# The first pass of a two-layer graph kernel: another order of the same steps within a slot

## The chip, the cores and the metric

One Trainium2 chip, one core of it. The metric is the time of one launch in device microseconds (us), measured outside of the profile. Several launches are timed and their median is compared.

## What is computed

Two graph layers follow each other over one graph of 3125 nodes and 103125 edges, which are sorted by destination. The change lies in the first, an attention layer with 4 heads of 32 channels:

```python
q = (x @ Wq.T + bq).reshape(N, H, C)
k = (x @ Wk.T + bk).reshape(N, H, C)
v = (x @ Wv.T + bv).reshape(N, H, C)
alpha = jnp.sum(q[dst] * k[src], axis=-1) / np.sqrt(C)
m = jax.ops.segment_max(alpha, dst, num_segments=N)
e = jnp.exp(alpha - m[dst])
z = jax.ops.segment_sum(e, dst, num_segments=N)
a = e / z[dst]
msg = a[:, :, None] * v[src]
out = jax.ops.segment_sum(msg, dst, num_segments=N)
```

Dense layers and norms follow, and then a second layer, which gathers rows again, weighs them with a small network of the edge's length and direction, and sums them by destination. All is in 32-bit floats.

## The kernel before

**Parts.** A short start makes tables of queries and of keys and values in device memory. The *first pass* goes over the edges for the attention layer. Then come the dense layers, then the *second pass* over the edges, and the end. The change touches the first pass alone.

**Tiles and slots.** An edge tile is 128 edges, a quad four tiles (`QT = 4`), and there are 202 quads (`NQ`). Every engine runs its own loop over *slots* `q`, one quad entering in each, and the engines meet at semaphores. A quad goes through this:

- GpSimd gathers the keys and values of its edges' sources (line 436, four gathers of 128 rows each) into a ring of 16 buffers. A buffer is filled again once VectorE has weighed the quad in it.
- SyncE loads the query rows of the quad's destinations (line 342, `windows`: edges are sorted, so 128 rows from the tile's first destination do), four slots ahead, once the queries of four slots ago are done. Every seventh slot it also stores a piece of a radial embedding for the second pass (line 364), for which it waits for an exponential of ScalarE (line 816).
- ScalarE makes one-hot matrices, edge by destination within the window (`make_hots`, lines 735 and 738: four squares and one Relu), three slots ahead.
- TensorE turns them (`turn_hots`, line 484, four transposes), two slots ahead; ScalarE copies the result out of PSUM (`turned`, line 749, into `hotT`); TensorE multiplies them with the query rows (`queries`, line 493), one slot ahead.
- VectorE multiplies queries and keys (`product`, line 1015) and adds up each head's 32 channels (`scores`, line 1025) into `alpha`.
- Quads form batches of eight, of four near the end. When a batch is complete, a chain of small steps works out each destination's maximum and the exponentials. It is spread over four slots, `step` 0 to 3 (`chain_at`): a transpose, two scans and the masks (step 0), two small transposes and scans over a row (step 1), twelve tiny matmuls and two scans (step 2), an exponential and a transpose back (step 3). ScalarE then copies the probabilities out (line 802).
- Twelve slots after it entered (`weighed(q)`), a quad is weighed: ScalarE spreads its probabilities over the channels (`spread`, line 758, into `exb`), and VectorE multiplies the values with them (`weigh`, line 1031, into `msg0`). In four slots (`DOUBLES`) and at the very end two quads are weighed.
- TensorE sums messages and probabilities by destination with the one-hots (`sums`, line 502: eight matmuls of 128x128, two for a tile), into one of two pairs of PSUM banks, and VectorE adds each tile's sums to the accumulator (`add_tile`, line 1046). `added(q)` are the quads weighed in the slot before.

A 32-bit matmul of 128 columns leaves two rows in the trace, a transpose one.

**The order in a slot, before.** Each engine works in the order in which its loop is written. TensorE: sums of the quads weighed in the slot before; the chain's step 0, 1 or 2; turns for slot `q + 2`; queries for slot `q + 1`; the chain's step 3. ScalarE: step 3's exponential; turned copy; small copies of steps 1 and 2; spread; one-hots; copy of the probabilities. VectorE: product; then per quad add 0, scores, add 1, weigh, add 2, the chain's step, add 3.

`sums` waits for `msg_ready` (the weighing) and for `acc_step` (VectorE's adds out of the same PSUM banks two quads ago). `queries` waits for the turned copy, for SyncE's windows and for the product of two quads ago (`prod_ready`). `turn_hots` waits for the one-hots and for the last turned copy.

## Time and profile before

| | |
|---|---|
| median of 3 runs | 3034.0 us (3033.17 to 3050.24) |
| the profiled execution | 3050.12 us |
| its span, first to last instruction | 3048.3 us |
| mean granted TensorE clock | 0.806 |
| first pass, steady stretch | 186 to 1480 us |
| second pass | about 1700 to 2980 us |

The profile is one execution. PE is TensorE's matmuls and PEld its weight loads, DVE is VectorE, ACT ScalarE, POOL GpSimd, SP SyncE. A row names the line, the engine, the operation, the tiles written and read, and what the engine waited for before it (`[5.49 <-remote]`: it stood idle for 5.49 us, and the profile does not know what ended that). "issue" is a wait for which the profile shows nothing. Ends of matmuls are modelled. The granted clock is 1 at 2.4 GHz and 0.5 at 1.2 GHz.

### The profile page before, as it was taken

Reading aid. Unit: us, or ns where it says so; the run is one execution under the profiler, and the core shown is the slowest. Engines: PE = TensorE matmul, PEld = TensorE weight load, DVE = VectorE, ACT = ScalarE, POOL = GpSimd, SP = SyncE. Lnnn points to the kernel's source line nnn. Section 1 sums busy time; section 2 is a strip of 40 time slices with the busy share of each in tenths; the row PEclk is TensorE's granted clock in tenths of the full one; section 3 lists DMA queues with packets and bytes.
Section 4 is the critical chain, followed back from the end, with each engine's and each line's share of the span. In section 5 each row is a group of like instructions: output and inputs, shape, how many; then the busy total and the mean of one; then the engine's idle time right before and its main releaser. Section 6 shows DMA issues by size and latency. Waiting matters only on the chain. (4 is left out here: it accounts for less than half of the span.)

```text
span 3048.3 us, 43625 instructions
## 1 busy us (share of the span) xinstructions
PE 2125.3 (70%) x12777; PEld 1763.9 (58%) x12777; DVE 1697.7 (56%) x4672; ACT 1216.2 (40%) x3032; POOL 1567.9 (51%) x1618
## 2 busy tenths in 40 slices
PE   4266666666666666656688178888888888888886
PEld 3255555565555566555676156666666666666665
DVE  2455555555555555555755055665666665666666
ACT  1344444444444444433435033333343333334344
POOL 4345555555555555545202756665666566656630
PEclk7588888878888878888888578787887777878788
DMA  6344444444343444434201211111111111111110
GB/s 219 86 113 120 120 122 120 117 121 121 113 124 112 124 122 114 115 106 123 77 5 31 52 37 45 45 45 42 46 47 45 42 44 44 45 42 45 46 28 22
DMA packets 212127, 243.01 MB, mean 80 GB/s; under 512 B 42992, under 2 KB 170022, under 8 KB 211508
## 3 DMA queue, kind: packets, MB, share of 16 engines
q0 software_dynamic: 64480, 158.57, 18.8%
q1 hardware_dynamic: 147412, 81.66, 9.3%
q8 instruction: 105, 1.72, 0.2%
q14 instruction: 130, 1.06, 0.1%
HBM read 228.12 MB, written 11.94 MB: 79 GB/s over the span
## 5 line engine op out<-in xcount | busy, mean ns | idle before, releaser
L436 POOL DMA_INDIRECT rows<-kv_tab,src_col x806 | 762.9, 947 | 712.3 <-DVE msg L1031 482.2
L451 POOL DMA_INDIRECT rows<-up_tab,src_col x806 | 791.9, 982 | 520.1 <-DVE hots L1308 272.6
L502 PE MATMUL ps<-hots,msg 128*128 128x128 f32 x1616 | 410.8, 344 | 493.1 <-DVE msg L1031 433.9
L699 PE MATMUL ps<-hotT,hots 128*128 128x128 f32 x3232 | 550.6, 340 | 260.4 <-DVE hots L1315 202.9
L699 PEld LDWEIGHTS ps<-hotT,hots 128*128 128x128 f32 x3232 | 504.2, 246 | 293.1 <-DVE hots L1315 219.1
L502 PEld LDWEIGHTS ps<-hots,msg 128*128 128x128 f32 x1616 | 314.9, 242 | 535.0 <-DVE msg L1031 480.5
L1279 DVE TENSOR_TENSOR acc<-acc,ps 128x256 f32 x808 | 336.6, 417 | 398.1 <-remote 225.1
L749 ACT COPY hotT<-ps 128x512 f32<-128x512 f32 x202 | 118.2, 585 | 815.4 <-remote 434.1
L1046 DVE TENSOR_TENSOR acc<-acc,ps 128x256 f32 x808 | 334.3, 414 | 130.9 <-remote 75.2
L502 PE MATMUL ps<-hots,exb 128*128 128x128 f32 x1616 | 386.3, 329 | 0.0
L1031 DVE TENSOR_TENSOR msg<-rows,exb 128x512 f32<-128x512 f32 x202 | 142.6, 706 | 424.6 <-ACT exb L758 289.9
L502 PEld LDWEIGHTS ps<-hots,exb 128*128 128x128 f32 x1616 | 318.0, 244 | 0.0
L688 PEld LDWEIGHTS ps<-weights,hots 64*128 64x128 f32 x1616 | 208.2, 198 | 104.4 <-issue 104.4
L493 PE MATMUL ps<-qwin,hotT 128*128 128x128 f32 x1616 | 247.8, 302 | 16.9 <-issue 11.6
L735 ACT ACTIVATE hots<-consts,nrel 128x128 f32<-128x128 f32 x808 | 257.6, 391 | 0.0
L735 ACT ACTIVATE hotT<-consts,nrel 128x128 f32<-128x128 f32 x808 | 255.6, 389 | 2.9 <-PE ps L699 2.9
L907 ACT ACTIVATE hots<-ps,vecs 128x512 f32<-128x512 f32 x101 | 69.4, 687 | 460.8 <-PE ps L678 170.7
L688 PE MATMUL ps<-weights,hots 64*128 64x128 f32 x1616 | 248.8, 297 | 5.8 <-issue 5.8
L493 PEld LDWEIGHTS ps<-qwin,hotT 128*128 128x128 f32 x1616 | 231.0, 219 | 18.1 <-issue 17.9
L901 ACT ACTIVATE hots<-ps,vecs 128x512 f32<-128x512 f32 x101 | 69.4, 687 | 378.2 <-PE ps L672 144.7
L1015 DVE TENSOR_TENSOR work<-ps,rows 128x512 f32<-128x512 f32 x202 | 138.0, 683 | 134.2 <-remote 113.5
L484 PE MATMUL ps<-consts,hots 128*128 128x128 f32 x808 | 148.6, 315 | 73.2 <-ACT hots L738 72.4
(163 smaller groups left out, 2569.7 us busy)
## 6 DMA issues: line engine op xcount, KB each, us to landing
qwin<-q_tab SPq DMA_DIRECT2D x808, 64.0 KB
rows<-kv_tab,src_col POOLq DMA_INDIRECT x806
rows<-up_tab,src_col POOLq DMA_INDIRECT x806
hots<-emb_rows SPq DMA_DIRECT2D x202, 16.0 KB
weights<-r_far SPq DMA_DIRECT2D x25, 128.0 KB
emb_rows<-weights SPq DMA_DIRECT2D x25, 128.0 KB
kv_tab<-rows SPq DMA_DIRECT2D x12, 256.0 KB, 2.8
dst_lanes<-in_dst_lanes SPq DMA_DIRECT2D x30, 65.0 KB
```

What stands on the lines that cost most here:

```text
L436: nc.gpsimd.indirect_dma_start(kvr[:, q % RING, k, :], None, kv_tab, bass.IndirectOffsetOnAxis(src_col[:, t:t + 1].bitcast(U32), 0)).then_ ...
L451: nc.gpsimd.indirect_dma_start(upr[:, q % RING, k, :], None, up_tab, bass.IndirectOffsetOnAxis(src_col[:, t:t + 1].bitcast(U32), 0)).then_ ...
L484: mm = pe.transpose(ps[:, 0, k * P:(k + 1) * P], hot_of[:, q % HOTS, k, :], ident)
L493: mm = pe.matmul(ps[:, 1 + q % 2, k * P:(k + 1) * P], hotT[:, q % 2, k, :], qwin[:, q % 4, k, :], start=True, stop=True)
L502: mm = pe.matmul(ps[:, 4 + 2 * (j % 2) + k // 2, (2 * (k % 2) + m) * P:(2 * (k % 2) + m + 1) * P], left[:, j % 2, k, :], hot_of[:, j % HOT ...
L688: mm = pe.matmul(ps[:, 2 + q % 2, k * P:(k + 1) * P], h2s[64 * half:64 * half + 64, u, k * P:(k + 1) * P], weights[64 * half:64 * half + 6 ...
L699: mm = pe.matmul(ps[:, 4 + 2 * (q % 2) + k // 2, (2 * (k % 2) + m) * P:(2 * (k % 2) + m + 1) * P], left[:, q % 2, k, :], hot2[:, q % 2, k, ...
L735: op = nc.scalar.activation(to[:, k, :], iota, ACT.Square, bias=nrel[:, q * QT + k:q * QT + k + 1])
L1015: v.tensor_tensor(work[:, q % 2, :].rearrange("p (t f) -> p t f", t=QT), ps[:, 1 + q % 2, :].rearrange("p (t f) -> p t f", t=QT), kvr[:, q ...
L1031: v.tensor_tensor(msg0[:, j % 2], kvr[:, j % RING, :, D:2 * D], exb[:, j % 2], ALU.mult).then_inc(msg_ready, 1)
L1046: v.tensor_tensor(to, to, ps[:, 4 + 2 * (j % 2) + k // 2, (k % 2) * 256:(k % 2) * 256 + 256] .rearrange("p (m f) -> p m f", m=2), ALU.add) ...
L1279: v.tensor_tensor(to, to, ps[:, 4 + 2 * (q % 2) + k // 2, (k % 2) * 256:(k % 2) * 256 + 256] .rearrange("p (m f) -> p m f", m=2), ALU.add) ...
```

## The change

The order of the steps within a slot is another on three engines, in the first pass only. Which quad is in which slot stays.

- ScalarE spreads ahead of the turned copy.
- VectorE weighs first, then adds tile 0, then the product, add 1, scores, add 2, step 0 of the chain, add 3, steps 1 and 2 of the chain.
- TensorE does queries and turns first, then the chain's steps, then the sums, and these are of the quads weighed in this slot (`weighed(q)`), not in the one before.
- The sums wait for the adds out of their PSUM banks pair by pair, where one wait stood for all four tiles.

```diff
--- before.py
+++ after.py
@@ -495,9 +495,9 @@
 
             def sums(j):
                 pe.wait_ge(msg_ready, j + 1)
-                if j >= 2:
-                    pe.wait_ge(acc_step, adds_before(j - 1))
                 for k in range(QT):
+                    if j >= 2 and k % 2 == 0:
+                        pe.wait_ge(acc_step, adds_before(j - 1) - QT + k + 2)
                     for m, left in enumerate((msg0, exb)):
                         mm = pe.matmul(ps[:, 4 + 2 * (j % 2) + k // 2, (2 * (k % 2) + m) * P:(2 * (k % 2) + m + 1) * P],
                                        left[:, j % 2, k, :], hot_of[:, j % HOTS, k, :], start=True, stop=True)
@@ -522,8 +522,10 @@
             one = ident[0:1, 0:1]
             for q in range(-2, LAST_SLOT):
                 b, step = chain_at(q)
-                for j in added(q):
-                    sums(j)
+                if 0 <= q + 1 < NQ:
+                    queries(q + 1)
+                if q + 2 < NQ:
+                    turn_hots(q + 2)
                 if step == 0:
                     pe.wait_ge(score_ready, STOPS[b])
                     if pads_to(b):
@@ -544,13 +546,11 @@
                         pe.matmul(lanes[:, 3 * P + 1:3 * P + 2], row_bw[0:1, HS * h + 2:HS * h + 2 + BT], one, start=True, stop=True)
                         mm = pe.matmul(lanes[:, 3 * P + 2:3 * P + 3], grown[0:1, 1, h:h + 1].to_broadcast([1, C]), one, start=True, stop=True)
                     mm.then_inc(back_mm, 1)
-                if q + 2 < NQ:
-                    turn_hots(q + 2)
-                if 0 <= q + 1 < NQ:
-                    queries(q + 1)
                 if step == 3:
                     pe.wait_ge(ex_ready, b + 1)
                     pe.transpose(ps[:, 3, 0:P], scr[:], ident).then_inc(probs_mm, 1)
+                for j in weighed(q):
+                    sums(j)
                 if q in (NQ + 1, NQ + 3):
                     prepare((q - NQ) // 2)
 
@@ -777,6 +777,8 @@
                 if step == 3:
                     act.wait_ge(shift_ready, b + 1)
                     nc.scalar.activation(scr[:], scr[:], ACT.Exp, scale=1.0 / np.sqrt(C).item()).then_inc(ex_ready, 1)
+                for j in weighed(q):
+                    spread(j)
                 if q + 2 < NQ:
                     turned(q + 2)
                 if step == 1:
@@ -791,8 +793,6 @@
                                          scale=-1.0 / np.sqrt(C).item()).then_inc(shrink_ready, 1)
                     nc.scalar.copy(tile_max[0:1, 0, :].rearrange("p (h t) -> p h t", h=H)[:, :, 0],
                                    row_fw[0:1, :].rearrange("p (h t) -> p h t", h=H)[:, :, BT]).then_inc(carry_sb, 1)
-                for j in weighed(q):
-                    spread(j)
                 if q + 3 < NQ:
                     make_hots(q + 3)
                 if step == 3:
@@ -1099,30 +1099,32 @@
 
             for q in range(LAST_SLOT):
                 b, step = chain_at(q)
-                if q < NQ:
-                    product(q)
                 if q in STARTS and shorter(batch_of(q)):
                     pad_lanes(batch_of(q))
                 adding, weighing = added(q), weighed(q)
                 for n in range(max(len(adding), len(weighing), 1)):
                     j = adding[n] if n < len(adding) else None
+                    if n < len(weighing):
+                        weigh(weighing[n])
                     if j is not None:
                         base = bases(j)
                         if j in STARTS[1:]:
                             shrink_first(j, base)
                         add_tile(j, 0, base)
                     if n == 0 and q < NQ:
+                        product(q)
+                    if j is not None:
+                        add_tile(j, 1, base)
+                    if n == 0 and q < NQ:
                         scores(q)
                     if j is not None:
-                        add_tile(j, 1, base)
-                    if n < len(weighing):
-                        weigh(weighing[n])
-                    if j is not None:
                         add_tile(j, 2, base)
-                    if n == 0 and step is not None:
+                    if n == 0 and step == 0:
                         chain(b, step)
                     if j is not None:
                         add_tile(j, 3, base)
+                    if n == 0 and step in (1, 2):
+                        chain(b, step)
                 if q == 2:
                     v.memset(acc[:, 1, :], 0.0).then_inc(acc_zero, 1)
                 if q == 4:
```

On TensorE, before, in plain slots in the middle of the first pass (L502 sums, L484 turns, L493 queries, L553 the chain's step 3):

```order
L484 MATMUL ps<-consts,hots 128x128 x4
L493 MATMUL ps<-qwin,hotT 128x128 x4
L553 MATMUL ps<-consts,scr 128x128
L502 MATMUL ps<-hots,msg 128x128
L502 MATMUL ps<-hots,exb 128x128
L502 MATMUL ps<-hots,msg 128x128
L502 MATMUL ps<-hots,exb 128x128
L502 MATMUL ps<-hots,msg 128x128
L502 MATMUL ps<-hots,exb 128x128
L502 MATMUL ps<-hots,msg 128x128
L502 MATMUL ps<-hots,exb 128x128
L484 MATMUL ps<-consts,hots 128x128 x4
```

and in the changed kernel (the chain's step 3 is there L551):

```order
L493 MATMUL ps<-qwin,hotT 128x128 x4
L484 MATMUL ps<-consts,hots 128x128 x4
L551 MATMUL ps<-consts,scr 128x128
L502 MATMUL ps<-hots,msg 128x128
L502 MATMUL ps<-hots,exb 128x128
L502 MATMUL ps<-hots,msg 128x128
L502 MATMUL ps<-hots,exb 128x128
L502 MATMUL ps<-hots,msg 128x128
L502 MATMUL ps<-hots,exb 128x128
L502 MATMUL ps<-hots,msg 128x128
L502 MATMUL ps<-hots,exb 128x128
L493 MATMUL ps<-qwin,hotT 128x128 x4
```

The sums came first and turns and queries behind them. Now queries stand ahead of the turns, and the chain's transpose ahead of the sums of its own slot; in a row of slots the sums still alternate with the pair.

On ScalarE, before, in two plain slots (L749 turned copy, L758 spread, L735 and L738 one-hots):

```order
L749 COPY hotT<-ps 128x512
L758 COPY exb<-probs 128x512
L735 ACTIVATE hots<-consts,nrel 128x128 x4
L738 ACTIVATE hots<-hots 128x512
L749 COPY hotT<-ps 128x512
L758 COPY exb<-probs 128x512
L735 ACTIVATE hots<-consts,nrel 128x128 x4
L738 ACTIVATE hots<-hots 128x512
```

and in the changed kernel:

```order
L758 COPY exb<-probs 128x512
L749 COPY hotT<-ps 128x512
L735 ACTIVATE hots<-consts,nrel 128x128 x4
L738 ACTIVATE hots<-hots 128x512
L758 COPY exb<-probs 128x512
L749 COPY hotT<-ps 128x512
L735 ACTIVATE hots<-consts,nrel 128x128 x4
L738 ACTIVATE hots<-hots 128x512
```

The spread was behind the turned copy and now stands ahead of it.

On VectorE, before, one plain slot (L1015 product, L1005 the load of the tiles' first destinations, L1046 add, L1025 scores, L1031 weigh; ISA rows are register work):

```order
L1015 TENSOR_TENSOR work<-ps,rows 128x512
L1005 TENSOR_LOAD base_i
L1046 ISA
L1046 TENSOR_TENSOR acc<-acc,ps 128x2x128
L1025 TENSOR_REDUCE alpha<-work 128x4x4
L1046 ISA
L1046 TENSOR_TENSOR acc<-acc,ps 128x2x128
L1031 TENSOR_TENSOR msg<-rows,exb 128x512
L1046 ISA
L1046 TENSOR_TENSOR acc<-acc,ps 128x2x128
L1046 ISA
L1046 TENSOR_TENSOR acc<-acc,ps 128x2x128
```

and in the changed kernel:

```order
L1031 TENSOR_TENSOR msg<-rows,exb 128x512
L1005 TENSOR_LOAD base_i
L1046 ISA
L1046 TENSOR_TENSOR acc<-acc,ps 128x2x128
L1015 TENSOR_TENSOR work<-ps,rows 128x512
L1046 ISA
L1046 TENSOR_TENSOR acc<-acc,ps 128x2x128
L1025 TENSOR_REDUCE alpha<-work 128x4x4
L1046 ISA
L1046 TENSOR_TENSOR acc<-acc,ps 128x2x128
L1046 ISA
L1046 TENSOR_TENSOR acc<-acc,ps 128x2x128
```

The weighing went from the slot's third quarter to its start, and the product from the start to behind the first add.

## Rows read from the trace of the kernel before

**Rows 1.** The page, busy time by engine, and the costliest group on GpSimd.

```profile
PE 2125.3 (70%) x12777; PEld 1763.9 (58%) x12777; DVE 1697.7 (56%) x4672; ACT 1216.2 (40%) x3032; POOL 1567.9 (51%) x1618
...
L436 POOL DMA_INDIRECT rows<-kv_tab,src_col x806 | 762.9, 947 | 712.3 <-DVE msg L1031 482.2
```

**Rows 2.** Stretches: busy us of each engine, granted clock, DMA share, GB/s.

```profile
186.00:1480.00 1294.00, 809.40 (x5793) 761.00 (x5794) 706.56 (x1643) 568.99 (x1469) 686.65 (x727) 0.84 0.41 118
...
2300.00:2900.00 600.00, 502.82 (x2511) 370.03 (x2511) 362.27 (x1116) 230.16 (x558) 365.59 (x372) 0.79 0.17 44
```

**Rows 3.** Line 749 from 186 to 1480 us: count, durations, first and last start.

```profile
L749 ACT COPY hotT<-ps x180: 585/585/586, 185.9 to 1477.4; 128x512 f32<-128x512 f32 x180
```

**Rows 4.** Waits from 186 to 1480 us: who for whom, us, times, longest.

```profile
PE ps L502 <- DVE msg L1031: 412.0, 160, 6.0
...
ACT hotT L749 <- remote: 381.1, 82, 10.1
...
DVE msg L1031 <- ACT exb L758: 281.9, 93, 8.3
...
ACT hotT L749 <- PE ps L484: 263.8, 82, 5.4
...
POOL rows L436 <- issue: 180.8, 566, 1.2
```

**Rows 5.** Timeline of a slot at full clock: start us, us, engine, line.

```profile
440.54 0.49 PE L502 MATMUL ps<-hots,msg 128*128 128x128 f32 x2 [2.95 <-DVE msg L1031]
...
442.42 0.60 PE L484 MATMUL ps<-consts,hots 128*128 128x128 f32 x4
...
443.57 0.58 ACT L749 COPY hotT<-ps 128x512 f32<-128x512 f32 x1 [1.58 <-PE ps L484]
...
444.05 0.62 ACT L758 COPY exb<-probs 128x512 f32<-128x512 f32 x1
...
445.45 0.49 PE L502 MATMUL ps<-hots,msg 128*128 128x128 f32 x2 [1.53 <-DVE msg L1031]
```

**Rows 6.** Timeline of a slot at the half clock.

```profile
384.82 0.80 PE L502 MATMUL ps<-hots,msg 128*128 128x128 f32 x2 [2.95 <-DVE msg L1031]
...
388.39 1.06 PE L484 MATMUL ps<-consts,hots 128*128 128x128 f32 x4
...
391.37 0.49 PE L502 MATMUL ps<-hots,msg 128*128 128x128 f32 x2 [0.30 <-DVE msg L1031]
```

**Rows 7.** Timeline of the slot after that of rows 5.

```profile
452.31 0.42 DVE L1046 TENSOR_TENSOR acc<-acc,ps 128x256 f32 x1 [3.03 <-remote]
...
452.39 0.58 ACT L749 COPY hotT<-ps 128x512 f32<-128x512 f32 x1 [5.49 <-remote]
```

**Rows 8.** Timeline of ScalarE before any sums.

```profile
117.17 0.58 ACT L749 COPY hotT<-ps 128x512 f32<-128x512 f32 x1 [15.86 <-remote]
...
120.80 0.58 ACT L749 COPY hotT<-ps 128x512 f32<-128x512 f32 x1 [1.21 <-PE ps L484]
```

**Rows 9.** Timeline of TensorE in a slot with a chain step ahead of the turns.

```profile
805.72 0.80 PE L502 MATMUL ps<-hots,msg 128*128 128x128 f32 x2 [4.29 <-DVE msg L1031]
...
813.75 0.50 PE L502 MATMUL ps<-hots,msg 128*128 128x128 f32 x2 [2.06 <-DVE msg L1031]
```

**Rows 10.** Chain of waits in the second pass: start us, us, what.

```profile
2410.27 3.79 PE ps L699 x16
...
2417.35 3.56 another core or an unknown queue
...
2423.63 3.80 PE ps L699 x16
```

**Rows 11.** SyncE's queue: its wait, one window's issue, landing of a larger table piece.

```profile
SPq L364 <- ACT weights L816: 281.6, 21, 20.1
...
448.02 0.53 SPq L342 DMA_DIRECT2D qwin<-q_tab  x1
...
kv_tab<-rows SPq DMA_DIRECT2D x12, 256.0 KB, 2.8
```


## The prediction

> **What bounds the kernel now.** I read the page first: no engine is busy for more than 70% of the span, and TensorE's row is the largest [rows 1]. So a sum of work does not set the end; a ring of waits may. Next I cut out the stretch in which the first pass is steady, 186 to 1480 us [rows 2]. There VectorE is busy 707 us of 1294, ScalarE 569, GpSimd 687, TensorE 809 (its records overlap, so that is too much), at a granted clock of 0.84. Half-full engines on all sides: they wait for each other.
>
> How long one slot takes comes from a count: the turned copy (line 749) runs once a slot, 180 times from 185.9 to 1477.4 us [rows 3]. That is 1291.5 us in 179 periods, 7.2 us a slot.
>
> The waits tell who waits [rows 4]. TensorE's sums stand 412 us behind VectorE's weighing (line 1031), the weighing stands 282 us behind ScalarE's spread (line 758), and ScalarE's turned copy 264 us behind TensorE's turns (line 484), plus 381 us put down to "remote". That is a closed ring: sums, turns, turned copy, spread, weigh, next sums. It can be walked in one plain slot at full clock [rows 5]: the sums start at 440.54, the turns at 442.42 (1.88 us), the turned copy starts at 443.57 (1.15 more), the spread at 444.05 (0.48), and the next sums, with the weighing between, at 445.45 (1.40). Period 4.91 us, of which 1.88 + 1.15 wait for TensorE and 1.88 us lie between turned copy and next sums, with TensorE left only its queries. In a slot at the half clock [rows 6] the sums take 3.57 us up to the turns and the period is 6.55 us.
>
> A third kind of slot matters [rows 7]: the next sums began at 445.45, so by the 3.03 us of the slot before the turned copy was due at 448.5. It starts at 452.39, after 5.49 us idle, and VectorE's first add of the same slot's sums, due well before, starts only at 452.31. Both engines are released together, so TensorE's results came some 4 us later than the same work took a slot before. The row names "remote", no engine. I call this a late finish. I do not know its cause, so I carry it along unchanged, and it is my main doubt.
>
> **The change part by part.** No instruction is added or taken away; the four parts move the links of the ring.
>
> Spread ahead of the turned copy (ScalarE), weighing first in the slot (VectorE): the spread now needs only its probabilities and a free exb buffer, and comes right after the last slot's one-hots. It no longer waits for the turns. Weighing and sums follow within 1.40 us, while TensorE does queries and turns. So the 412 us of waiting for the weighing lose their cause, except where other links are as long.
>
> Queries, then turns, then sums (TensorE): in a row of slots this is still sums, then the other two, but queries come before turns, and the chain's small steps stand behind the turns instead of ahead of them. Queries now wait for a turned copy of the slot before, 1.88 us of sums earlier, which covers it.
>
> What is late next, at full clock? One ring is left with ScalarE: turns, turned copy, one-hots, next turns. The trace shows it alone, in the slots before any sums exist: copies at 117.17 and 120.80, so 3.63 us [rows 8]. TensorE's own issue is 1.88 for the sums, 0.44 for the turns, and about 0.95 for the queries (recorded 1.06), 3.3 us. VectorE's busy time is 707 us over 179.4 slots, 3.9 us. Since these records overlap, its floor is some tenths less, and I take 3.6 for the slot. Gain at full clock: 4.91 - 3.6 = 1.3 us. At the half clock TensorE becomes the bound itself: 3.57 for the sums, turns at twice 0.44, queries at some 1.7, 6.15 us against 6.55, a gain of 0.4 us.
>
> The granted clock of 0.84 lies between 1 (2.4 GHz) and 0.5 (1.2 GHz), so about two thirds of the time are at full clock [rows 2]. The change works on the 190 slots 12 to 201. Sum: 190 x (2/3 x 1.3 + 1/3 x 0.4) = 190 us.
>
> VectorE's product moves behind the weighing and one add, and its queries two slots on wait for it. The weighing's 0.7 and the add's 0.4 delay it, while TensorE has 1.88 us of sums to do; I cost it at nothing. If the sums' cover were gone, the price would be 1.1 us x 190 = 209 us. The finer acc_step waits (one per pair of tiles) let sums start up to two adds earlier; those adds are done a slot before, so nothing either way.
>
> The chain of maxima (29 batches that lie beside other slots): ahead of the turns its steps cost ring time. A slot with one (step 1) takes 8.03 us at the half clock, 805.72 to 813.75 [rows 9], 1.5 us over the plain 6.55. For two such slots that is 3 us a batch. Behind the turns they leave the ring. Against that, steps 1 and 2 of VectorE's chain now end the slot, and the next slot's small matmuls stand ahead of the sums and wait for them; and step 3's exponential stands ahead of the spread as before. The price lies between -3 us a batch (all gained) and +3 us (two steps of about 1.4 us in the open); I take a gain of 0.7, 29 x 0.7 = 20 us. Both ends together are 87 us either way.
>
> Total: 190 + 20 = 210 us. The profiled execution took 3050.1 us (its span 3048.3); that gives 2840. The median of the runs shown is 3034.0, 16 lower, so 2824.
>
> GpSimd's gathers are the next floor. One costs 0.947 us and 180.8/566 = 0.32 us of issue [rows 1, 4], four of them 5.07 us a slot. My slots of 3.6 us are faster than that, yet half-clock slots of 6.15 and late finishes bring the mean to 7.2 - 210/190 = 6.1, and the ring of 16 buffers, refilled four slots ahead, evens it out.
>
> **The rivals.**
>
> A. The gathers become the bound. If TensorE's pauses go, the clock could stay at full and the late finishes vanish. Then a slot is 5.07 us: 190 x (7.2 - 5.07) = 405 us, 2629. For it speaks that the clock is low after long pauses: two sums' records take 0.80 us behind 4.29 us of idleness and 0.49 to 0.50 behind 1.53 and 2.06 us (behind 2.95 us both are found) [rows 5, 6, 9]. Against it speaks the second pass, in which TensorE's records fill 503 of 600 us and the clock granted is 0.79, lower than in the first pass with its pauses [rows 2]. The Trainium skill ("TensorE: Matmul & The Clock Gate", section "HAM oscillation — how this bites in real kernels") says that idle gaps between bursts of matmuls throw the clock back to its half and that closing them keeps it up; by that rule this rival is the case, and the trace agrees only in part.
>
> B. The late finishes set TensorE's pace. In the second pass they come again and again: two slots take 13.36 us (2410.27 to 2423.63) and one piece of 3.56 us in each such pair has no known releaser [rows 10]. That is 6.68 us a slot in a pass that has little more work for TensorE. If the first pass is driven into the same pace, 190 x (7.2 - 6.68) = 99 us, 2935. For it: same late pieces, same rows. Against: the slot of 4.91 us has no such piece in it [rows 5].
>
> C. Slower: the queries' rows come late. The window rows (qwin) are loaded by SyncE once the queries four slots back are done. Every seventh slot SyncE first stands for the exponential of the radial embedding, 281.6 us in 21 waits, 13.4 us each [rows 11]. Then the store is issued, and behind it the windows, four to a slot, 0.53 us each [rows 11]. Queries now stand first in the slot, and four slots shrink from 29 to 24 us. If the waits came into the open, each of the 26 stores would stall queries, turns and sums. It decides the sign from 210/26 = 8.1 us each; at the full 13.4 us it is +348 - 210 = +138 us, 3172. Against it: the exponential belongs to a slot three ahead of the one that needs the windows behind it, so some two and a half slots, 15 us, are there for four issues of 0.53 us and a landing (a larger piece of a table lands after 2.8 us [rows 11]), some 5 us.
>
> D. It does little: the sums' wait of 412 us goes, but the 381 us of "remote" waits [rows 4] grow by as much, because TensorE is held by its own late finishes whatever the order. Then the gain stays under 30 us, 3010. Against it: slots without a late finish have no such thing in them.
>
> **How the numbers follow.** Forecast 0.60, its own range 2740 to 2900; A 0.12; B 0.20; C 0.05; D 0.03. A measurement of this kernel tells about 1% from no change. Faster by over 1%: nearly all of the forecast, A and B, less tails, 0.89. Within 1%: D and a bit of B's tail, 0.05. Slower 0.06: C, and the cover of the product gone. The 8-in-10 range reaches to B's far side, 2960, and down to 2690, between forecast and A; what is left out is most of A, C and D.
>
> **What would show it.** Right: in the plain slots the spread starts within 0.1 us behind the one-hots' Relu, the copies at full clock are 3.6 to 4 us apart, at half clock 6.2; waits of the sums for the weighing under 150 us; the first pass ends some 210 us sooner, and the second takes the same time. Wrong towards A: GpSimd's waits for the weighing near nothing and the clock above 0.9. Towards B: the sums of the "remote" waits grow, and the mean slot is above 6.5. Towards C: TensorE idle ahead of the queries every seventh slot. The forecast falls if the mean slot stays above 6.8 us.

## The result and the profile after

| | kernel before | changed kernel |
|---|---|---|
| median, measured together | 3034.93 us (3033.17 to 3050.24, 4 runs) | 3077.24 us (3069.61 to 3088.38, 4 runs) |
| ratio, 95% interval | 1 | 1.0131 [1.0085, 1.0177] |
| profiled execution, span | 3050.12, 3048.3 us | 3074.52, 3072.7 us |
| mean granted clock | 0.806 | 0.783 |

The change made the kernel 1.3% slower, where 210 us of gain were forecast. First the page of the changed kernel, its busy times and GpSimd's two groups of gathers.

```profile
PE 2197.1 (72%) x12777; PEld 1795.0 (58%) x12777; DVE 1695.0 (55%) x4672; ACT 1216.1 (40%) x3032; POOL 1582.0 (51%) x1618
...
L436 POOL DMA_INDIRECT rows<-kv_tab,src_col x806 | 774.7, 961 | 731.4 <-DVE msg L1031 477.9
L451 POOL DMA_INDIRECT rows<-up_tab,src_col x806 | 794.5, 986 | 506.3 <-DVE hots L1310 259.7
```

The counts are those of [rows 1]: the same work. The stretches of [rows 2] in the changed kernel:

```profile
186.00:1480.00 1294.00, 860.09 (x5633) 773.67 (x5633) 681.94 (x1593) 554.21 (x1430) 680.87 (x708) 0.78 0.40 114
```

In the same 1294 us every engine gets through fewer instructions (TensorE 5633 for 5793, VectorE 1593 for 1643), at a granted clock of 0.78 for 0.84. Who waits for whom, against [rows 4] (us in total, times, longest):

```profile
ACT hotT L749 <- remote: 595.7, 89, 9.1
POOL rows L436 <- DVE msg L1031: 414.8, 90, 7.2
DVE msg L1031 <- ACT exb L758: 326.6, 93, 8.5
POOL rows L436 <- issue: 198.1, 618, 1.7
...
PE ps L493 <- ACT hotT L749: 142.2, 30, 6.6
...
PE ps L502 <- DVE msg L1031: 17.5, 26, 2.6
```

The wait that the change was to remove is gone: the sums' wait for the weighing was 412.0 us and is 17.5. But the turned copy's waits for "remote" grew from 381.1 to 595.7 us. The timeline shows what such a wait is now, with GpSimd's gathers beside it:

```profile
443.66 0.58 ACT L749 COPY hotT<-ps 128x512 f32<-128x512 f32 x1 [6.75 <-remote]
...
447.74 0.59 ACT L749 COPY hotT<-ps 128x512 f32<-128x512 f32 x1 [0.75 <-PE ps L484]
...
447.98 0.94 POOL L436 DMA_INDIRECT rows<-kv_tab,src_col  x1 [5.38 <-DVE msg L1031]
...
450.54 0.60 PE L484 MATMUL ps<-consts,hots 128*128 128x128 f32 x4
450.99 0.69 DVE L1031 TENSOR_TENSOR msg<-rows,exb 128x512 f32<-128x512 f32 x1 [0.55 <-PE ps L502]
...
451.73 0.95 POOL L436 DMA_INDIRECT rows<-kv_tab,src_col  x1 [0.30 <-issue]
451.74 0.49 PE L502 MATMUL ps<-hots,msg 128*128 128x128 f32 x2 [0.60 <-issue]
...
456.73 0.95 POOL L436 DMA_INDIRECT rows<-kv_tab,src_col  x1 [0.30 <-issue]
457.21 0.58 ACT L749 COPY hotT<-ps 128x512 f32<-128x512 f32 x1 [6.25 <-remote]
...
457.85 2.07 PE L493 MATMUL ps<-qwin,hotT 128*128 128x128 f32 x8 [4.06 <-issue]
...
461.53 0.94 POOL L436 DMA_INDIRECT rows<-kv_tab,src_col  x1 [3.85 <-DVE msg L1031]
```

Read it by the weighings, since each one frees a buffer and so starts four gathers. Here the turns stand in the records at 447.10 and 450.54, 3.44 us apart, so the quick slot of the forecast exists (its turned copy at 447.74 comes promptly). Two weighings follow each other faster than four gathers (5 us) are issued, and GpSimd issues eight in one row without a pause, 447.98 to 457.68. The turns recorded at 450.54 are over at 451.14, but the copy of their result starts at 457.21, 6.1 us later, when the row is nearly over. Everything else has stopped by then.

I counted this for each turned copy from 186 to 1000 us: its start less the recorded end of the turns before it, and of that what is over 0.5 us (the "late sum"). For the kernel before it is 143 us over 115 slots of 7.03 us, for the changed one 323 us over 112 slots of 7.31 us. So a slot holds 1.24 us of late finish before and 2.88 after, and the rest of it is 5.79 us before and 4.43 after. By this count the ring gave 1.4 us a slot, and the late finishes took 1.6. The count is an estimate, not a measurement of the two apart: lateness that shows elsewhere than ahead of the turned copy is in the rest.

The traces also hold the moments at which TensorE's semaphores count up, though no view prints them. The turns' semaphore counted up at 457.19, and the copy started 0.02 us later. So do all 31 copies in the kernel before that are more than 2.5 us late, and 52 of 53 in the changed one: what is late is TensorE's own signal, not a reader of it and not a window of the queries. And signals come in bunches. The four tiles' sums from 451.74 us signalled at 459.33, 459.39, 459.45 and 459.51. Signals of the sums 0.06 us apart occur 39 times from 186 to 1000 us before and 132 times in the changed kernel, but never in e5, e12 and e15 below, where the shortest distance is 0.445 us. A tile's sums that take at least 0.445 us there were hardly done in 0.06 here, so in these bunches TensorE's work was over and its signals were held back.

### The profile page after: what moved, and what is told of

It reads as the page before. It is cut to its first block and busy times, and to the rows that moved or that the text cites. A ratio compares the mean times of both kernels' runs of the same rounds, so it can differ in the third digit from the quotient of the medians.

```text
span 3072.7 us, 43625 instructions
## 1 busy us (share of the span) xinstructions
PE 2197.1 (72%) x12777; PEld 1795.0 (58%) x12777; DVE 1695.0 (55%) x4672; ACT 1216.1 (40%) x3032; POOL 1582.0 (51%) x1618
## 3 DMA queue, kind: packets, MB, share of 16 engines
q14 instruction: 131, 1.07, 0.1%
## 5 line engine op out<-in xcount | busy, mean ns | idle before, releaser
L436 POOL DMA_INDIRECT rows<-kv_tab,src_col x806 | 774.7, 961 | 731.4 <-DVE msg L1031 477.9
L493 PE MATMUL ps<-qwin,hotT 128*128 128x128 f32 x1616 | 305.2, 349 | 367.4 <-issue 184.1
L493 PEld LDWEIGHTS ps<-qwin,hotT 128*128 128x128 f32 x1616 | 273.2, 255 | 389.0 <-issue 210.5
L502 PE MATMUL ps<-hots,msg 128*128 128x128 f32 x1616 | 396.3, 330 | 94.1 <-issue 47.2
L749 ACT COPY hotT<-ps 128x512 f32<-128x512 f32 x202 | 118.2, 585 | 816.5 <-remote 677.6
L502 PE MATMUL ps<-hots,exb 128*128 128x128 f32 x1616 | 373.5, 316 | 29.4 <-issue 28.6
L1046 DVE TENSOR_TENSOR acc<-acc,ps 128x256 f32 x808 | 334.6, 414 | 105.2 <-PE ps L502 40.8
L502 PEld LDWEIGHTS ps<-hots,msg 128*128 128x128 f32 x1616 | 301.7, 231 | 144.2 <-issue 71.3
L1031 DVE TENSOR_TENSOR msg<-rows,exb 128x512 f32<-128x512 f32 x202 | 142.6, 706 | 404.2 <-ACT exb L758 344.0
L502 PEld LDWEIGHTS ps<-hots,exb 128*128 128x128 f32 x1616 | 300.7, 230 | 35.9 <-issue 35.6
L735 ACT ACTIVATE hots<-consts,nrel 128x128 f32<-128x128 f32 x808 | 257.6, 391 | 0.0
L735 ACT ACTIVATE hotT<-consts,nrel 128x128 f32<-128x128 f32 x808 | 255.5, 389 | 2.9 <-PE ps L699 2.9
L484 PE MATMUL ps<-consts,hots 128*128 128x128 f32 x808 | 164.4, 340 | 32.4 <-ACT hots L738 20.4
L1015 DVE TENSOR_TENSOR work<-ps,rows 128x512 f32<-128x512 f32 x202 | 138.0, 683 | 81.4 <-remote 68.6
```

The lines of the kernel that those rows point to most:

```text
L436: nc.gpsimd.indirect_dma_start(kvr[:, q % RING, k, :], None, kv_tab, bass.IndirectOffsetOnAxis(src_col[:, t:t + 1].bitcast(U32), 0)).then_ ...
L484: mm = pe.transpose(ps[:, 0, k * P:(k + 1) * P], hot_of[:, q % HOTS, k, :], ident)
L493: mm = pe.matmul(ps[:, 1 + q % 2, k * P:(k + 1) * P], hotT[:, q % 2, k, :], qwin[:, q % 4, k, :], start=True, stop=True)
L502: mm = pe.matmul(ps[:, 4 + 2 * (j % 2) + k // 2, (2 * (k % 2) + m) * P:(2 * (k % 2) + m + 1) * P], left[:, j % 2, k, :], hot_of[:, j % HOT ...
L735: op = nc.scalar.activation(to[:, k, :], iota, ACT.Square, bias=nrel[:, q * QT + k:q * QT + k + 1])
L1015: v.tensor_tensor(work[:, q % 2, :].rearrange("p (t f) -> p t f", t=QT), ps[:, 1 + q % 2, :].rearrange("p (t f) -> p t f", t=QT), kvr[:, q ...
```

## The experiments

The runs fell on two chips, 13 and 3. On chip 13 the kernel before takes 3033 us in one group of runs and 3103 in another (e9's expectation takes these for two chips), on chip 3 it takes 2284 to 2287 us. For the pair of the result no chip is on record; its 3035 us and its late finishes are those of chip 13, and it is counted there. Each group of runs was measured together with the kernel before on its own chip, and ratios are only of that. Letters in the expectations name theories, which they explain; late finishes of 236 and 503 us there are sums over the whole steady stretch. "Late" is the late sum from 186 to 1000 us, "slot" the mean distance of turned copies there.

| run | chip | this, us | before, us | ratio, 95% interval | slot, us | late, us |
|---|---|---|---|---|---|---|
| e1 | 13 | 3101.27 | 3103.11 | 0.998 [0.994, 1.002] | 7.32 | 237 |
| e2 | 13 | 3104.69 | 3103.11 | 1.000 [0.997, 1.003] | 7.08 | 123 |
| e3 | 13 | 3252.29 | 3103.11 | 1.046 [1.040, 1.052] | 7.93 | 85 |
| e4 | 13 | 3137.04 | 3103.11 | 1.012 [1.009, 1.015] | 7.43 | 271 |
| e5 | 3 | 2141.7 | 2286.22 | 0.936 [0.930, 0.941] | 4.42 | 18 |
| e6 | 3 | 2295.61 | 2286.22 | 1.003 [1.001, 1.005] | 5.20 | 28 |
| e7 | 3 | 2290.6 | 2286.22 | 1.002 [1.000, 1.003] | 5.21 | 9 |
| e8 | 3 | 2288.53 | 2286.22 | 1.000 [0.999, 1.002] | 5.19 | 27 |
| e9 | 13 | 3083.34 | 3033.25 | 1.013 [1.008, 1.018] | 7.27 | 308 |
| e10 | 13 | 3065.17 | 3033.25 | 1.012 [1.008, 1.016] | 7.23 | 270 |
| e11 | 13 | 3087.71 | 3033.25 | 1.017 [1.012, 1.022] | 7.27 | 305 |
| e12 | 13 | 2540.7 | 3033.25 | 0.837 [0.834, 0.840] | 4.40 | 19 |
| e13 | 3 | 2203.57 | 2287.44 | 0.964 [0.962, 0.966] | 4.76 | 0 |
| e14 | 3 | 2141.92 | 2287.44 | 0.938 [0.935, 0.941] | 4.42 | 18 |
| e15 | 3 | 2287.28 | 2287.44 | 1.000 [0.999, 1.002] | 5.17 | 24 |
| e16 | 3 | 2288.93 | 2287.44 | 1.001 [1.000, 1.003] | 5.18 | 24 |
| e17 | 3 | 2285.09 | 2284.29 | 1.001 [1.000, 1.002] | 5.15 | 23 |
| e18 | 3 | 2144.24 | 2284.29 | 0.940 [0.938, 0.943] | 4.43 | 18 |

**The parts of the change alone (e1 to e4).** e1 is the kernel before with ScalarE's part, e2 with VectorE's, e3 with TensorE's (order and finer wait), e4 the changed kernel with turns ahead of queries.

```diff
# e1, ScalarE (the spread behind the small copies goes)
+                for j in weighed(q):
+                    spread(j)
                 if q + 2 < NQ:
                     turned(q + 2)
...
-                for j in weighed(q):
-                    spread(j)
# e2, VectorE (and the adds and the chain as in the change)
-                if q < NQ:
-                    product(q)
...
+                    if n < len(weighing):
+                        weigh(weighing[n])
# e3, TensorE (and the finer wait as in the change)
-                for j in added(q):
-                    sums(j)
+                if 0 <= q + 1 < NQ:
+                    queries(q + 1)
+                if q + 2 < NQ:
+                    turn_hots(q + 2)
...
+                for j in weighed(q):
+                    sums(j)
# e4, on the changed kernel
+                if q + 2 < NQ:
+                    turn_hots(q + 2)
                 if 0 <= q + 1 < NQ:
                     queries(q + 1)
-                if q + 2 < NQ:
-                    turn_hots(q + 2)
```

> The kernel before with ScalarE's part alone: the spread ahead of the turned copy. Theory L (load: TensorE's results come late when sums, turns and queries follow each other without a pause): the weighing comes up to 1.2 us sooner in a slot, the pauses shrink, and late finishes grow part of the way from the 236 us of before (sum of turned copy's start behind the recorded end of the turns, over 0.5 us) towards the 503 us of the changed kernel; time 3035 to 3060. Theory O (order: turns now stand behind queries, so that a late query holds up the ring): turns are still ahead of queries, late finishes stay near 236 us and the time falls, to 2900 to 3000.

> The kernel before with VectorE's part alone: weighing first, product behind the first add. The spread still waits for the turned copy, so VectorE stands at the weighing with product and scores behind it, and queries of two slots on wait for that product. Both theories: TensorE's order and the ring are the old ones, time 3035 to 3120, late finishes no more than before; a loss would be the delayed product, up to 1.1 us in 190 slots.

> The kernel before with TensorE's part alone: queries, turns, chain, sums. The spread waits for the turned copy as before, so the pauses ahead of the sums stay. Theory O: late queries now delay the turns, the turned copy, the spread and the weighing, so this is the slowest of the three, 3090 to 3200, with late finishes above 400 us. Theory L: pauses as before, late finishes near 236 us, time 3035 to 3080, the queries' 0.9 us added in the ring of each slot at most (190 x 0.9 = 171 us).

> The changed kernel with turns ahead of queries, all else as changed. Theory O: turns are back ahead of the queries and the gain forecast shows, 2830 to 2950, late finishes under 300 us. Theory L: TensorE is packed as tightly as in the changed kernel, time 3050 to 3090, late finishes near 500 us, still in every second slot.

ScalarE's and VectorE's parts alone change nothing that can be measured, TensorE's alone costs 4.6%, and the order of turns and queries does not matter (1.012 for e4, 1.013 for the changed kernel in its own two groups). That speaks against theory O. Theory L failed too, in e3, which it put at 3080 us at most.

e1 shows more than its ratio. A *row* of gathers is a run of them without a pause over 0.65 us. Rows are 5.3 us long on average in the kernel before, 12 of 104 over 6 us. In e1's trace they are 9.8 us, 54 of 56 over 6 us, and the late sum is 237 us. So the spread ahead of the turned copy alone joins the rows and lengthens the late finishes, with TensorE's order the old one. The traced run is the slowest of e1's nine (3132.94 us), and over all nine e1 costs nothing that can be measured. e2 keeps short rows (5.4 us) and has 123 us.

e3 is worth a look as well. It has few late finishes (85 us) and the longest slot. Its timeline:

```profile
448.03 0.69 DVE L1031 TENSOR_TENSOR msg<-rows,exb 128x512 f32<-128x512 f32 x1 [3.87 <-ACT exb L758]
...
448.99 0.95 POOL L436 DMA_INDIRECT rows<-kv_tab,src_col  x1 [3.48 <-DVE msg L1031]
...
452.75 0.95 POOL L436 DMA_INDIRECT rows<-kv_tab,src_col  x1 [0.30 <-issue]
452.92 0.87 PE L484 MATMUL ps<-consts,hots 128*128 128x128 f32 x4
...
454.77 0.58 ACT L749 COPY hotT<-ps 128x512 f32<-128x512 f32 x1 [4.94 <-PE ps L484]
...
456.16 0.69 DVE L1031 TENSOR_TENSOR msg<-rows,exb 128x512 f32<-128x512 f32 x1 [3.24 <-ACT exb L758]
```

Here a slot can be walked through GpSimd: the weighing at 448.03 frees the buffer, four gathers run from 448.99 to 453.70, the turned copy starts 1.07 us behind them, spread and weighing follow at once. Period 8.1 us. In all 27 slots of e3 with a copy more than 2.5 us late, GpSimd was issuing gathers when the turns' records ended, or had stopped within 0.3 us of it, and in the middle eight tenths of them the copy came 1.0 to 1.2 us after the row of gathers was over. In the kernel before there are 31 such slots, and there it is 1.0 to 1.9 us. No row of e3 is over 6 us. It is slow in another way: weighing, gathers, turned copy and spread follow one another in each slot. That made the gathers the suspect (theory D below).

**No gathers, no windows, a lighter TensorE, chip 3 (e5 to e8).** All on the changed kernel. e5 leaves out the first pass's gathers behind quad 16, e6 the queries' windows, e7 half of the sums' columns, e8 multiplies zeros in the sums.

```diff
# e5, also e12 (and e13 on the kernel before); VectorE's waits for rows are cut to match
-                if q >= RING:
-                    pool.wait_ge(msg_ready, q - RING + 1)
-                for k in real_tiles(q):
+                for k in (real_tiles(q) if q < RING else []):
# e6; the queries' wait for windows ends with quad 3
             for q in range(NQ):
-                windows(q)
+                if q < 4:
+                    windows(q)
+                else:
+                    sp.wait_ge(qe_ready, q - 3)
# e7, also e10; n is the number of columns of each of the sums' matmuls
+                        n = P // 2 if 20 <= j < 180 else P
...
# e8, also e11
-                                       left[:, j % 2, k, :], hot_of[:, j % HOTS, k, :], start=True, stop=True)
+                                       zero[:] if 20 <= j < 180 else left[:, j % 2, k, :], hot_of[:, j % HOTS, k, :], start=True, stop=True)
```

> The changed kernel with the first pass's gathers left out from quad 16 on (products and messages then use old rows). Theory L (load: TensorE's own dense work makes its results late): the late finishes stay, about 500 us in sum, mean slot 7.2 to 7.5 us. Theory D (data: traffic of the gathers into SBUF holds TensorE's reads or writes up): late finishes fall below 100 us and the mean slot to 4 to 5 us, 500 us less in all.

> The changed kernel with SyncE's window loads left out from quad 4 on (queries then use old windows). Theory L: as changed, mean slot 7.2 to 7.5 us, late finishes about 500 us. Theory W (the queries really wait for windows, and what the records call a late finish is that wait): late finishes go, mean slot 4 to 5 us.

> The changed kernel with the sums' matmuls of quads 20 to 179 cut from 128 to 64 columns (half of each tile's sums is not computed). TensorE's work in a slot falls from 3.2 to 2.3 us at full clock. Theory L: late finishes fall by more than the 0.9 us saved, mean slot to 5.0 to 5.6 us, 250 to 350 us less in all. Theories D and W: only what the sums take goes, late finishes stay at 2.5 us or more a slot, mean slot 6.5 to 7 us.

> The changed kernel with the weights of the sums' matmuls of quads 20 to 179 replaced by zeros (those sums are then zero), same instructions, same waits. Theory L1 (the load is electrical and depends on what is multiplied): late finishes fall clearly, mean slot under 6.5 us. Theory L2 (the load is counted in instructions or columns): nothing changes, mean slot 7.2 to 7.5 us.

This chip was a surprise: it has hardly any late finish, with any kernel, and the kernel before takes 2286 us there. With gathers the slot is 5.2 us whatever else is left out, without them 4.42. That is rival A's bound (four gathers, 5.07 us) as a fact. In e8 GpSimd issues gathers from 186 to 1000 us without a pause over 0.32 us, one row of 632, and nothing is late. So a long row alone does not make a late finish; it takes a chip like 13. What e6, e7 and e8 were to tell of the late finishes, they cannot tell here.

**The same on chip 13 (e9 to e12).** e9 is the changed kernel as it is; e10, e11 and e12 are the edits of e7, e8 and e5.

> The changed kernel once more, as the base of this call. Chips differ: the kernel before took 3035 and 3103 us on two and 2286 us on a third, where no late finish was seen. On a chip of the first kind, both theories: 0.5 to 2% slower than before, late finishes about 500 us. On one of the third kind: the slot is bound by the four gathers (4 x 1.27 = 5.1 us) in both kernels, ratio 0.99 to 1.01, although nothing in the ring is late.

> As e7 (half of each tile's sums of quads 20 to 179 left out). Where results come late: theory L (TensorE's own load) mean slot 5.1 to 6.2 us against 7.4, 200 us or more less than the changed kernel; theory D (the gathers' traffic) only some 0.9 us a slot less, 6.5 to 6.9 us. Where they do not: bound by gathers, the same time as the changed kernel within 1%.

> As e8 (zero weights in the sums of quads 20 to 179). Where results come late: L1 (electrical load, depends on the numbers) mean slot under 6.6 us and 120 us or more less; L2 (counted in instructions or columns) as the changed kernel within 1.5%; theory D as L2. Where they do not: same time as the changed kernel.

> As e5 (no gathers from quad 16 on in the first pass). Where results come late: theory L mean slot 7 us or more, late finishes as in the changed kernel; theory D late finishes under 100 us and slots of 4.4 us, as on the chip of e5. Where they do not: 140 to 150 us less than the changed kernel, as in e5.

Half of the sums' columns moves the ratio from 1.013 to 1.012, with intervals that overlap almost wholly; zeros give 1.017 in two runs, which is not clear of 1.013; without gathers 543 us are gone (2540.7 against e9's 3083.34) and with them the late finishes, 308 us down to 19. That is theory D's forecast (under 100 us, slots of 4.4 us) and not theory L's. The stretches of e9 and of e12:

```profile
186.00:1000.00 814.00, 542.71 (x3551) 490.01 (x3550) 425.84 (x985) 353.23 (x905) 431.10 (x448) 0.77 0.41 116
```

```profile
186.00:1000.00 814.00, 689.72 (x5937) 639.62 (x5937) 713.06 (x1690) 576.42 (x1485) 6.92 (x1) 0.95 0.26 73
```

In the same 814 us TensorE does 5937 matmul records for 3551, VectorE 1690 instructions for 985, and the granted clock is 0.95 for 0.77, with *more* work on TensorE. The waits of e12 have no "remote" on the turned copy (line 747 there):

```profile
ACT hotT L747 <- PE ps L482: 151.8, 145, 3.7
```

Without the gathers the two chips are alike in the first pass: 4.40 us a slot on chip 13 (e12), 4.42 on chip 3 (e5). What is left of the difference lies where both still gather. Of the 397 us between the two traces, 62 are there at the 13th turned copy (151.3 against 89.4 us), while the first 16 quads are gathered, and some 337 come from the second pass's first gather to the end. The gathers' own rows there, e12 first, then e5:

```profile
L449 POOL DMA_INDIRECT rows<-up_tab,src_col x806: 938/944/1320, 1147.6 to 2436.1; - x162
```

```profile
L449 POOL DMA_INDIRECT rows<-up_tab,src_col x806: 940/945/1326, 1087.8 to 2099.9; - x162
```

A gather's median record is as short on one chip as on the other (944 and 945 ns), yet the gathers take from 1147.6 to 2436.1, 1289 us, on the first and 1012 on the second (806 gathers at 1.25 us from start to start: 1008). Nor do their transfers differ: from 200 to 1000 us they take 25.3% of the DMA engines' time for 56.91 MB in the changed kernel on chip 13, and 36.3% for 81.44 MB in e15 on chip 3, the same per byte. So the chips hardly differ in the gathers' speed. They differ in what goes on beside them.

**The kernel before without gathers, and other gathers (e13 to e18).** e13 is the edit of e5 on the kernel before. e14 and e18 gather two of four tiles. In e15 and e17 the second pair of gathers waits for the sums of the quad whose buffer it fills, in e16 all four do.

```diff
# e14, e18; VectorE's waits for rows are cut to match
+        def first_tiles(q):
+            return real_tiles(q) if q < RING else range(min(2, len(real_tiles(q))))
...
-                for k in real_tiles(q):
+                for k in first_tiles(q):
# e15, e17 (k == 2) and e16 (k == 0)
                 for k in real_tiles(q):
+                    if q >= RING and k == 2:
+                        pool.wait_ge(sum_ready, QT * (q - RING + 1))
```

> The kernel before, in which the first pass gathers its first 16 quads only and works on with the rows that are there (left out: the other gathers of the first pass, so its output is another). The changed kernel so cut took 0.837 of the kernel before, 4.40 us a slot. Theory D (the changed order does shorten the ring, the gathers take it back): this one walks its old ring, some 4.9 to 5.0 us a slot, 190 x 0.5 = 95 us more, ratio 0.86 to 0.88. Rival N (the changed order is worth nothing even alone): 0.83 to 0.845, slot 4.4 us. On a chip without late finishes both kernels stand at 2286 us and the changed one without gathers at 0.936; then D gives 0.97 to 0.98, N 0.936.

> The changed kernel with two of the four gathers of each quad from the 17th on in the first pass (the other two rows of tiles are old ones, so its output is another). Theory R (a late finish needs a long unbroken row of gathers): GpSimd has 2.5 us of issue a slot, rows of two with pauses between, so the late finishes go almost wholly (sum in 186 to 1000 us under 60 us against 308), slot 4.4 to 4.8, ratio 0.84 to 0.86. Rival S (each gather costs its share): halfway between 1.013 and 0.837, 0.92 to 0.93. On a chip without late finishes: slot 4.4, 0.94 by both.

> The changed kernel with nothing left out; gathers 3 and 4 of a quad wait for the end of the sums of the quad whose buffer they fill, so that GpSimd pauses inside a quad. Theory R: rows of at most some 2.5 us, results come out in the pauses; late finishes in 186 to 1000 us under 150 us (308), slot under 6.6 us, ratio 0.93 to 0.98. Rival S (only the number of gathers counts): 1.01 as before this edit. On a chip without late finishes the pause costs time, since the gathers are the bound there: 1.00 to 1.05.

> The changed kernel with nothing left out; all four gathers of a quad wait for the end of the sums of the quad whose buffer they fill. Theory R: rows of 5 us stay, but two quads in one row get rare since each group waits for a result of TensorE's; late finishes fall less than with pairs, 150 to 250 us, ratio 0.97 to 1.00. Rival S: 1.01. A third, C2: the gathers then lie on TensorE's queries and turns each time and hold those up in every slot: slot over 7.5 us, ratio over 1.03.

> The same kernel as e15 (nothing left out, gathers 3 and 4 of a quad wait for the sums of the quad whose buffer they fill). On a chip where the kernel before takes over 3000 us, theory R: late finishes in 186 to 1000 us under 150 us (308 in the changed kernel), slot under 6.6 us, ratio 0.93 to 0.98; rival S: ratio 1.01, late finishes near 300 us. On a chip of some 2290 us: 1.000 again, which tells nothing.

> The same kernel as e14 (two of the four gathers of a quad left out from the 17th quad on in the first pass). On a chip where the kernel before takes over 3000 us, theory R: late finishes in 186 to 1000 us under 60 us, slot 4.4 to 4.8, ratio 0.84 to 0.86; rival S: 0.92 to 0.93. On a chip of some 2290 us: 0.938 again.

Both groups fell on chip 3. So e14 to e18 tell nothing of the late finishes: theories R and S stay open, and whether pacing helps on chip 13 was not measured. They do show that half of the gathers cost no more than none (2141.92 and 2144.24 against e5's 2141.7). e15 and e16 did not pace anything: in e15 no pause ahead of a gather is over 0.32 us from 186 to 1000 us, since sums of 16 quads ago are long done when the gathers themselves are the bound.

e13 against e5 tells what the changed order is worth when nothing disturbs it: 2203.57 - 2141.7 = 62 us (the two come from two groups on chip 3, in which the kernel before agrees within 1.3 us). By slots it is the same: 4.76 - 4.42 = 0.34 us, times 186 slots that no longer gather, 63 us. ScalarE's timeline of e13, then of e5, over most of a batch:

```profile
601.09 0.58 ACT L747 COPY hotT<-ps 128x512 f32<-128x512 f32 x1 [1.69 <-PE ps L482]
...
606.44 0.58 ACT L747 COPY hotT<-ps 128x512 f32<-128x512 f32 x1 [2.16 <-PE ps L482]
...
624.26 0.58 ACT L747 COPY hotT<-ps 128x512 f32<-128x512 f32 x1 [1.47 <-PE ps L482]
...
628.67 0.58 ACT L747 COPY hotT<-ps 128x512 f32<-128x512 f32 x1 [1.46 <-PE ps L482]
```

```profile
602.19 0.59 ACT L747 COPY hotT<-ps 128x512 f32<-128x512 f32 x1 [0.80 <-PE ps L482]
...
607.12 0.31 ACT L777 ACTIVATE scr<-scr 128x128 f32<-128x128 f32 x1 [1.32 <-DVE scr L1090]
...
607.84 0.58 ACT L747 COPY hotT<-ps 128x512 f32<-128x512 f32 x1
...
613.76 0.59 ACT L747 COPY hotT<-ps 128x512 f32<-128x512 f32 x1 [2.70 <-PE ps L482]
...
620.89 0.59 ACT L747 COPY hotT<-ps 128x512 f32<-128x512 f32 x1 [1.03 <-PE ps L482]
...
624.56 0.59 ACT L747 COPY hotT<-ps 128x512 f32<-128x512 f32 x1 [0.75 <-PE ps L482]
```

A plain slot is 4.41 us before (624.26 to 628.67) and 3.67 after (620.89 to 624.56; the next two are 3.45 and 3.68). But the slots with chain steps are 5.65 and 5.92 us after (602.19 to 607.84 to 613.76), where before the longest is 5.35. Over a batch of eight slots the copies' distances add up to 36.7 us before and 34.1 after: the plain ring gives 8 x 0.74 = 5.9 us, and the chain takes 3.3 of it back.

## Why the prediction was wrong

**The step that failed** is the late finish: "I do not know its cause, so I carry it along unchanged, and it is my main doubt." It did not stay unchanged, it more than doubled (1.24 to 2.88 us a slot), and by that count its growth of 1.6 us alone turned the sign. What the runs show of it: it needs the gathers (e12 against e9), not the width of the sums or what they multiply (e10, e11), and not the order of turns and queries (e4). In the kernel before, a late copy comes 0.3 to 2.1 us behind the end of a row of gathers. In the changed kernel it is looser: from 2.6 us ahead of the row's end to 2.5 behind it in the middle eight tenths. The link to the change is the row's length. GpSimd's rows from 186 to 1000 us are 5.3 us long on average before, 12 of 104 over 6 us, and 8.5 us in the changed kernel, 47 of 64 over 6 us (e9: 9.4 us, 49 of 59). In e9, of the 61 turns whose records end inside a row 52 have a copy over 2.5 us late, of the other 51 only 2.

So the old ring was also a brake. With the spread behind the turned copy and a period of 5 us and more, weighings mostly came no faster than four gathers are issued, and each row of four ended before the next. Freed from the ring, two weighings come 3.6 us apart, their gathers join to a row of eight, ten microseconds long, all stops until it is over, and then two quick slots follow again. In the changed kernel 36 of 111 distances between turned copies are under 4 us and 44 over 9; before it was none of either. That part, row length as the cause, is argued and not shown. It rests on these counts, on the timelines and on the traces taken together: with short rows (before, e2, e3: 4.7 to 5.4 us) a slot holds 0.8 to 1.3 us of late finish, with long ones (e1, e4, e9, e10, e11, the changed kernel: 8.5 to 9.8 us) 2.1 to 2.9. Each of these runs changed the order of steps, and so more than the row length.

**The ring at full clock, 4.91 to 3.6 us.** The mechanism was right: the sums' wait went (412.0 to 17.5 us), and the plain slot is 3.67 us. The size was off: without gathers the old ring takes 4.41 us, so the slot of [rows 5] probably held half a microsecond of late finish already (GpSimd is issuing in it), and the term is 0.74 us, not 1.3. Over all slots the order gave 0.34 us undisturbed, where the forecast had 1.1.

**The chain's term** was to be a gain of 0.7 us a batch, within -3 and +3. It is a cost of 3.3 us a batch (e13 against e5), just past my bad end: the exponential of step 3 waits for the scans that moved to the end of VectorE's slot (`ACT L777`, 1.32 us), and spread and turned copy stand behind it. The prediction named both and then chose the side of a gain.

**The product behind the weighing, and the windows (rival C)** cost nothing that shows: e5's plain slot is as forecast, and e6 has no gain from leaving the windows out, though on chip 3 alone, where the gathers would hide one. On chip 13 the late copies start 0.02 us behind the turns' own signal, so they do not wait for windows.

**Rival A** was wrong for chip 13. On chip 3 its bound holds, 5.07 us forecast and 5.2 measured, but there the kernel before stands at it as well, so its gain of 405 us appears nowhere. Its premise, that the pauses go with the changed order and the late finishes with the pauses, has it the wrong way round as far as the runs go: the late finishes stayed and kept the pauses; when the gathers were taken away, late finishes and pauses went and the clock stood at 0.95. What the Trainium skill says of idle gaps ("TensorE: Matmul & The Clock Gate", "HAM oscillation — how this bites in real kernels") agrees with e12 against e9: TensorE has 35 pauses over 2.5 us in e9 at a clock of 0.77, and 4 in e12 at 0.95. e13 against e5 is no test of it, since each has one such pause from 186 to 900 us; closing the pauses over 1 us there (133 in e13, 6 in e5) did not raise the clock, which is 1.00 and 0.96.

**Rivals B and D** came nearest. D said that the "remote" waits grow by as much as the sums' wait shrinks, because TensorE is held by its late finishes whatever the order. They grew by 215 us, the sums' wait shrank by 395. But the prediction gave D 0.03 and let it end at a gain of 30 us: neither had a way in which a faster ring makes late finishes longer, and that was the sign.

**Open.** Whether the issue of gathers on GpSimd, their descriptors or their traffic holds TensorE's signals up, whether TensorE also runs late at times (ends of matmuls are modelled), why chip 13 does so and chip 3 does not, and whether gathers issued in pairs, or half of them, would free chip 13. Nothing complete beats the kernel before: with late signals the changed order loses 1.3%, and with prompt ones both orders end at the gathers. The changed kernel as it is did not run on chip 3; the nearest to it, e15 and e17, whose extra waits did nothing, stand at 1.000 and 1.001.

## What to carry to other kernels

A wait that no engine explains is a term of the sum like any other. If it cannot be sized for the changed kernel, first find what it goes along with (here: put the gathers' rows beside it in the timeline of the kernel before), because a change that reorders work also reorders that. A ring of waits can hold another engine's bursts apart: before it is shortened, ask which engine it paces and what happens if that one runs without a pause. And measure the floor with the suspect taken out: two runs without gathers gave the ring's undisturbed worth (62 us), and against them the 5.2 us of a slot with gathers is seen as a bound.

## What the runs showed of the hardware

- Two chips run the same kernel at 3033 to 3103 us and at 2284 to 2287 us. Where nothing is gathered they agree (4.40 and 4.42 us a slot). Beside gathers chip 13 counts the turns' semaphore up as much as 9.3 us behind the recorded end (changed kernel; 4.5 us in the kernel before, 186 to 1000 us); on chip 3 (e15), and on both without gathers (e12, e5), it is 0.01 to 0.02 us in every slot. A gather's median record is 944 ns on one and 945 ns on the other.
- Beside gathers the granted clock is 0.77 on chip 13 (e9) and 0.96 on chip 3 (e15), from 186 to 1000 us; without them it is 0.96 on both (e12 and e5, 186 to 900 us). A late finish occurs at full clock too: the matmuls from 451.74 us above start with a pair of 0.49 us, as the full-clock slot of [rows 5] does (0.80 us at the half clock, [rows 6]).
- Half of the sums' columns lowered the clock, on both chips: 0.69 (e10) against 0.77 (e9), and 0.81 (e7) against 0.97 (e8). In e7 no pause of TensorE is over 2.6 us.
